# Expert tiles: the gates and weighted LoRA rows move ahead of the preceding tile's epilogue

## The reference

```
logits = LN(x) @ W_router.T                          # 8 experts
p, i = top_k(softmax(logits), 2);  p = p / sum(p)
w = sum(one_hot(i) * p)                              # [rows, 8], two entries not zero
h = LN(x) @ lora_A                                   # [rows, 8, 16]
x = x + 0.5 * (LN(x) @ W_base.T + b_base + 2 * sum_e w_e * h_e @ lora_B_e)
```

## Time and profile before

| what | us |
|---|---|
| median of 3 runs | 1405.7 (1405.19 to 1406.45) |
| the profiled execution | 1411.57 |
| its span in the profile | 1409.8 |
| TensorE busy (matmuls) | 1286.9, 91% |
| VectorE busy | 943.4, 67% |
| ScalarE busy | 639.8, 45% |
| GpSimd busy | 483.3, 34% |

### The profile page before, as it was taken

The page is one execution under the profiler, slowest core; times in us unless marked ns, Lnnn a source line. Parts: engine busy times, 40 slices in busy tenths (PEclk is TensorE's granted clock), DMA queues, the critical chain, the costliest instruction groups (busy, mean ns, idle before and its releaser), DMA issues.

```text
span 1409.8 us, 21535 instructions
## 1 busy us (share of the span) xinstructions
PE 1286.9 (91%) x7392; PEld 824.5 (58%) x7392; DVE 943.4 (67%) x2782; ACT 639.8 (45%) x959; POOL 483.3 (34%) x733
## 2 busy tenths in 40 slices
PE   3988999999899998998979889999998999999988
PEld 1886543444268896444858854444432788954368
DVE  5664888999337944652857468889991587366356
ACT  1236266666632335444212544666665222544522
POOL 1574031221155542114626621321122554311162
PEclk9999588999999999899989976999999999989999
DMA  9200000001002001000140000000010100010001
GB/s 300 92 1 30 2 2 2 32 3 40 1 1 71 1 1 39 2 2 0 61 145 1 1 31 2 2 4 31 2 40 2 57 16 1 3 37 1 2 0 60
DMA packets 19420, 39.60 MB, mean 28 GB/s; under 512 B 4401, under 2 KB 5681, under 8 KB 19185
## 3 DMA queue, kind: packets, MB, share of 16 engines
q1 hardware_dynamic: 19312, 38.23, 8.0%
HBM read 32.33 MB, written 11.29 MB: 31 GB/s over the span
## 4 chain that ended last, share of the span: by engine, by line
PE 69%; DVE 16%; POOL 5%; issue 4%; ACT 4%; DMA 2%; SPq 0%; DVEq 0%; ACTq 0%; POOLq 0%
PE bank L781 16%; PE bank L674 12%; PE bank L596 8%; PE bank L598 7%; PE bank L597 7%; DVE maxes L980 5%; PE bank L765 4%; PE bank L654 4%; PE bank L759 3%; PE bank L576 3%; DVE unused L976 3%; PE bank L684 2%; POOL probs L1254 1%; DVE xT L844 1%; DVE gate L904 1%
## 5 line engine op out<-in xcount | busy, mean ns | idle before, releaser
L1180 ACT ACTIVATE probs<-bank 128x1024 f32<-128x1024 f32 (+3 forms) x416 | 367.9, 911 | 304.3 <-PE bank L765 195.6
L674 PE MATMUL bank<-ops 48*128 48x512 f32 (+3 forms) x960 | 321.0, 438 | 13.2 <-DVE maxes L980 3.8
L976 DVE CUSTOM_DVE_ANT_0 unused<-bank,causal 128x128 bf16<-128x128 f32 (+3 forms) x640 | 279.5, 486 | 73.9 <-PE bank L674 70.5
L1333 POOL TENSOR_SCALAR_AFFINE_SELECT probs<-probs 128x256 f32<-128x256 f32 (+1 forms) x256 | 118.8, 464 | 590.1 <-ACT probs L1180 589.9
L674 PEld LDWEIGHTS bank<-ops 48*128 48x128 f32 (+1 forms) x960 | 162.5, 207 | 198.2 <-DVE maxes L976 81.6
L781 PE MATMUL bank<-probs,v_mem 128*17 128x512 f32 (+6 forms) x1920 | 259.1, 531 | 6.1 <-ACT heads_raw L1169 5.6
L980 DVE TENSOR_REDUCE maxes<-bank 128x1 f32<-128x512 f32 x320 | 207.2, 684 | 38.0 <-PE bank L674 36.4
L1080 ACT CAST xT<-bank 128x512 fp32r<-128x512 f32 (+1 forms) x128 | 71.3, 560 | 280.5 <-PE bank L576 280.5
L844 DVE TENSOR_TENSOR xT<-bank,xT 128x512 fp32r<-128x512 f32 (+1 forms) x128 | 83.6, 656 | 148.4 <-ACT xT L1080 148.4
L765 PE MATMUL bank<-ops 50*128 50x512 f32 (+2 forms) x640 | 177.9, 454 | 4.1 <-ACT probs L1180 4.0
L596 PE MATMUL bank<-w_odd_hi,xT 128*128 128x384 f32 (+2 forms) x448 | 169.0, 377 | 2.1 <-DVE xT L844 1.9
(11 more groups left out here) (102 smaller groups left out, 1743.6 us busy)
## 6 DMA issues: line engine op xcount, KB each, us to landing
w_odd_lo<-staging_wqkv SPq DMA_DIRECT2D x4, 1536.0 KB, 6.7
x<-x_dram SPq DMA_DIRECT2D x16, 256.0 KB, 6.0
out_dram<-x SPq DMA_DIRECT2D x16, 256.0 KB, 2.0
staging_wqkv<-wqkv_dram SPq DMA_DIRECT2D x2, 1536.0 KB, 14.1
ops<-staging_dora SPq DMA_DIRECT2D x3, 1024.0 KB, 5.1
ops<-staging_base SPq DMA_DIRECT2D x2, 1296.0 KB, 6.4
w_odd_lo<-staging_base SPq DMA_DIRECT2D x2, 1296.0 KB, 5.8
ops<-shiftT SPq DMA_DIRECT2D x160, 4.0 KB
```

Of the source, the lines that this page charges most:

```text
L674: last = mm(dst[:, h * w:(h + 1) * w], queries(a, u)[rows, t // 4, hi, t % 4 * P:(t % 4 + 1) * P], keys(a, u, hi)[rows, HALF * kp:HALF * k ...
L976: V.tensor_tensor_reduce(unused[:, masked % 3, 0:w], part, causal[:, HALF - w:], 1.0, NEG, ALU.add, ALU.max, dst).then_inc(s["max_done"].s ...
L1180: A.activation(probs[:, e % 6, :, 0:cols], scores[:, 2 * (e % 2):2 * (e % 2) + 2, 0:cols], ACT.Exp, scale=a.scale).then_inc(s["exp"].sem, 1)
L1333: G.affine_select(out=p, in_=p, compare_op=ALU.is_ge, fill=0.0, base=0, pattern=pattern, channel_multiplier=-1).then_inc(s["masked"].sem, 1)
```

## The change

In VectorE's loop, `weigh` of tile i-1 is issued before `epilogue` of tile i-2 instead of after it. No instruction is added, removed or altered, and no wait or semaphore.

```diff
@@ -949,12 +949,12 @@
                         normalise(b, *its[i + 1])
                     if 3 <= i < len(its) + 3 and its[i - 3][0] in ATT:
                         rope_sum(b, *its[i - 3])
+                    if experts:
+                        weigh(b, *its[i - 1])
                     if 2 <= i < len(its) + 2:
                         epilogue(b, *its[i - 2])
                         if its[i - 2][0] in ATT:
                             rope_cos_part(b, *its[i - 2])
-                    if experts:
-                        weigh(b, *its[i - 1])
```

## The result

The changed kernel takes 1435.2 us (median of 6 runs, 1432.5 to 1445.2), the one before 1406.2 (6 runs, 1405.2 to 1414.1): ratio 1.0198, 95% interval 1.0157 to 1.0238, 29 us slower. The forecast was 1435.0.

What follows compares the result with a forecast made beforehand. In the expert stages TensorE and VectorE were both taken as near their limit, with VectorE often waiting for GpSimd. Stage terms 2 x 7.9 + 7.7 + 5.8 = 29.3 us, added to the median 1405.7, gave 1435.0; range 1419 to 1441.

Steps and rivals of the forecast that it cites:

- (1): VectorE's expert turns: L872 and L874, hidden under the wait for GpSimd before, come after L910, 0.66 us later.
- (2): TensorE's begin waits for the later x_new; the L844 of two turns on can't start before 6.05 us after L874's end.
- L837 loses its place: VectorE's L837 starts 2.89 us after L844, behind GpSimd's start at 2.42, and lasts 1.47 instead of 0.54.
- X: End of VectorE's L874 in a turn, counted from L844; forecast 5.61 us without a chunk, 7.12 with 768 columns.
- The edge turns: Turns where L837 comes hardly ahead of GpSimd: L874's end taken as 5.36 us after L844, four turns, 0.25 either way.
- GpSimd held behind L837: In turns with a chunk, L1235 put 0.23 us later because L837 has the port; bounds nothing and 0.31.
- The ends of the stages: TensorE's waits for the last hw go: 0.48 us in each MOE_A, 0.92 in each MOE_B.
- A: Rival: L837 keeps ahead of GpSimd or isn't held; +21.6 us, 1427; 18 in 100.
- B: Rival: TensorE's wait for x_new stays hidden; +7.5 us, 1413; 8 in 100.
- C: Rival: faster, weigh runs in VectorE's idle time ahead of L872; 2.8 us less, 1402.9; 4 in 100.
- D: Rival: nothing to measure, gains at stage ends against losses in a few turns; 1405.7 us; 3 in 100.
- E: Rival: TensorE's pauses bring its granted clock down in the expert stages; above 1441 us; 5 in 100.

Runs made afterwards that it cites:

- last_tile_only: Kernel before, with weigh ahead of epilogue only in the turn of tile 7 of each expert stage; 1405.2 us, ratio 0.9983.
- psum_norm_changed: Changed kernel, with the expert numbers read from PSUM and normalise (L837) put ahead of routing (L887); 1410.3 us, ratio 1.0020.
- psum_changed: Changed kernel, with the expert numbers that L899 and L904 read copied to a free PSUM bank; 1424.3 us, ratio 1.0108.
- changed_all_but_first: Changed kernel, with the new order in all tiles of an expert stage but the first; 1442.6 us, ratio 1.0234.
- gates_split: Kernel before, with only L898 and L899 of weigh moved ahead of the epilogue, the rest left behind it; 1422.4 us, ratio 1.0121.
- norm_first: Changed kernel, with normalise (L837) put ahead of routing (L887); 1435.8 us, ratio 1.0196.

## Why the prediction was right

The forecast of 29.3 us stands against 29.0 by the medians, 30.3 by the runs at equal clock and 30.4 by the stage sum: 7.9, 7.7, 7.9 and 5.8 by stage against 8.2, 7.6, 8.5 and 6.1. In each MOE_A 0.3 of this comes back in QKV1 (last_tile_only), so 29.8 remain. Step by step:

- **(1) The epilogue leaves its cover.** Right. Turn 0 moved L844 of turn 1 by 0.59 (4.98 long, 4.39 before); 0.60 was forecast.
- **(2) x_new and TensorE's loop.** Right; psum_norm_changed shows the loop without the port, 5.17 measured for (4.30 + 6.05)/2. L887 comes 2.29 behind L844 (forecast 2.30).
- **L837 loses its place.** Right in turns 1 to 4 of every stage and in most others. The turns of the changed kernel (those without a chunk from MOE_B of batch 1):

| | forecast | measured |
|---|---|---|
| turn, 768 columns | 7.04 | 6.99 |
| turn, 512 columns | 6.49 | 6.45 |
| X, no chunk, L837 caught | 5.61 | 5.62 |
| turn, no chunk, mean of three | 5.83 | 5.92 |

- **The edge turns.** The prediction took the middle of two cases; of the four turns of the change that lay on the edge one was free and three were caught. In MOE_A of batch 0 L837 got in 0.10 ahead of L1235, whose record is then 1.56 long instead of 1.28; in the same turn of batch 1 it lasted 1.63:

```profile
494.46 1.56 POOL L1235 TENSOR_TENSOR x<-x,bbase 128x512 f32<-128x512 f32 x1
...
494.36 0.54 DVE L837 TENSOR_SCALAR probs<-x,mv,rstd 128x512 f32<-128x512 f32 x1
...
1193.90 1.63 DVE L837 TENSOR_SCALAR probs<-x,mv,rstd 128x512 f32<-128x512 f32 x1
...
1193.98 1.27 POOL L1235 TENSOR_TENSOR x<-x,bbase 128x512 f32<-128x512 f32 x1
```

  L1235 is recorded 0.10 after L837 in the first and 0.08 after it in the second. The expert stages of all runs together show where it turns. GpSimd kept the port in all seven pairs in which L837 is recorded 0.06 to 0.09 ahead of it (L837 1.61 to 1.64 long; psum_changed, the change, changed_all_but_first). L837 kept it in both pairs at 0.10 and in the five at 0.15 to 0.32 (gates_split). The Trainium skill (SBUF — State Buffer, Who interferes with whom) lets whoever issues first keep the port; these rows agree only if a VectorE instruction's recorded start is counted 0.1 later against GpSimd's. The free case was also taken too short: the prediction has X = 5.11 there, and it measured 5.40, because L1235, held itself, ended later and L899 with it.
- **GpSimd held behind L837.** The term of 0.23 was a little too large: L1235 isn't recorded later but longer, 1.46 for 1.29, so 0.17, where 0.33 of L837 was left. In the edge turn 0.44 was left and L1235 grew by 0.28; in gates_split 0.22 and 0.07. GpSimd's record grew each time by 0.14 to 0.16 less than what was left, so it isn't held for all of the 0.31 that the prediction worked out from the Trainium skill's rule.
- **The ends of the stages.** The 0.92 of each MOE_B measured 1.1 and the 0.48 of each MOE_A 0.3 (last_tile_only), because L634 waits for the copy of hwT as well. The errors are 0.2 a stage and cancel.
- **The rivals.** A (L837 isn't held), B (x_new hidden), C and D (faster, no change) are refuted by the rows above. E did not happen in the change: the granted clock is 1.00 in its four windows with TensorE's pauses, and the mean clock of its six runs, 0.929 to 0.939, is no lower than that of before. That a fall can come in these stages, norm_first and changed_all_but_first show; it cost 1.7 and about 2 us, far from E's price. In norm_first TensorE had waited 1.89 for L879 just before the clock fell; in the same turn of batch 1 it waited 1.95, and the clock stayed. So the pauses aren't shown to be the cause.

What the prediction didn't see is that its mechanism feeds itself. The late state needs a first late X; the forecast put one in each turn anyway and so came out right, but the expectation of psum_changed, made with the same working, failed by 15 us in the stage sum on this.

Part of the closeness is luck: the turns with chunks were forecast 0.04 to 0.05 too long and the edge turns too short, and the two partly offset each other.

What stays open: where the 0.1 us between the recorded starts comes from, what brings the granted clock down in one expert stage and not in the next, and so how close to an edge turn a forecast can be.

## What to carry to other kernels

Before moving a short VectorE instruction, look at what GpSimd executes at its new place and what the instructions behind it lose as cover: an operation on eight columns that takes 0.28 us by itself lasted up to 1.86 (norm_first), and in gates_split, up to 1.77 long, it cost nothing in the turns that something else bound. In a software pipeline follow the moved result round the whole loop to its own next start, and ask both whether the late state sustains itself and whether the good state is ever reached. If the port is the trouble, change where an operand lies before changing the order: eight columns copied to PSUM gave 7 us.

When medians of a few runs and a sum of windows disagree, compare the granted clocks first: here 0.01 of mean clock was worth 8.9 us, as much as several of the effects.

## What I had not expected of the hardware

- An instruction of GpSimd that meets a VectorE instruction under way isn't recorded as starting later; its record grows: L1235 from 1.28 or 1.29 to 1.46, and to 1.56 in the edge turn, with L837's 0.54 in front of it. VectorE's record grows in the same way (0.54 to 1.63). A sum of busy times therefore contains the waits: VectorE's 17 us more.
- The same code took 421 to 432 us in different profiles, with granted clocks of 0.92 and 0.88. A change worth 0.5% is seen in chosen windows long before it is seen in the medians of whole runs, and in whole runs once the clock is taken out.
